# Experts' result rows in two halves by turns, stored from ScalarE's queue instead of SyncE's

## The reference, cut to what matters

```python
logits = x @ gate_w.T                      # 2048 tokens, 16 experts
vals, idx = jax.lax.top_k(softmax(logits), 2)
gate_out = (x @ g.T).reshape(bs, 16, 112)
up_out = (x @ u.T).reshape(bs, 16, 112)
h = jax.nn.silu(gate_out) * up_out
out = jnp.einsum('bei,hei,be->bh', h, d_r, w)
x = x + jnp.tanh(g_ffn[0]) * out
```

## Time and profile before

| what | value |
|---|---|
| median of three runs | 1417.61 us (1416.63 to 1420.79) |
| the profiled execution's own time | 1419.29 us |
| its span in the trace | 1417.6 us |
| busy PE, DVE, ACT, POOL | 89%, 55%, 39%, 41% |
| first down product of the experts to the last | 623.07 to 865.34 us, 39 tiles, 38 periods |

### The profile page before, as it was taken

How to read it: one execution, slowest core, us unless ns; L and a number is a source line. 1 busy time by engine, 2 the same in 40 slices (tenths; PEclk the granted TensorE clock), 3 DMA queues, 4 the chain that set the end, 5 groups by cost and what they waited for, 6 DMA issues and landing times. The chain is left out here.

```text
span 1417.6 us, 21035 instructions
## 1 busy us (share of the span) xinstructions
PE 1267.5 (89%) x6498; PEld 860.6 (61%) x6498; DVE 786.1 (55%) x2006; ACT 550.9 (39%) x913; POOL 579.5 (41%) x960
## 2 busy tenths in 40 slices
PE   3799999999976999999999994999999999658786
PEld 1354545445444854468777883888888889335443
DVE  2878888887863670023333333644554433449995
ACT  2544444444423400024343444232222232068884
POOL 4776868676732000012221222623222221157885
PEclk9999999999988999999999997999999999979999
DMA  5210212302003503038778865325323330121111
GB/s 192 78 71 30 89 59 94 128 30 104 0 1 139 221 1 125 21 95 260 253 224 260 270 211 192 119 91 133 106 90 120 120 90 31 59 68 45 59 59 74
DMA packets 52479, 156.36 MB, mean 110 GB/s; under 512 B 5952, under 2 KB 16192, under 8 KB 52288
## 3 DMA queue, kind: packets, MB, share of 16 engines
q1 hardware_dynamic: 39152, 113.60, 22.5%
q0 software_dynamic: 13264, 41.95, 10.7%
HBM read 113.06 MB, written 45.61 MB: 112 GB/s over the span
## 5 line engine op out<-in xcount | busy, mean ns | idle before, releaser
L1163 PEld LDWEIGHTS ex_bank<-ex_xT,ex_gu 128*112 128x112 f32 x1248 | 140.3, 177 | 25.2 <-issue 24.3
L1163 PE MATMUL ex_bank<-ex_xT,ex_gu 128*112 128x128 f32 x1248 | 144.0, 274 | 2.1 <-issue 1.0
L44 PE MATMUL xa_bank<-xa_fT_high,M_hi 128*128 128x256 f32 x512 | 145.6, 284 | 0.0
L45 PE MATMUL xa_bank<-xa_fT_low,M_hi 128*128 128x256 f32 x512 | 144.9, 283 | 0.0
L46 PE MATMUL xa_bank<-xa_fT_high,M_lo 128*128 128x256 f32 x512 | 144.9, 283 | 0.0
L52 PE MATMUL la_bank<-la_osum,la_tab 128*128 128x512 f32 x256 | 121.0, 618 | 15.8 <-POOL la_osum L297 14.6
L297 POOL TENSOR_TENSOR la_osum<-la_oprod 128x512 f32<-128x512 f32 x64 | 80.1, 1274 | 96.8 <-DVE la_oprod L476 96.8
L1051 POOL TENSOR_TENSOR ex_small<-listed,ex_small 128x1 int32<-128x1 int32 x42 | 8.0, 190 | 236.6 <-DVE Wk L1118 236.5
L1402 DVE SCALAR_TENSOR_TENSOR X<-ffn_row,weights,X 128x1024 f32<-128x1024 f32 x32 | 48.6, 1517 | 93.0 <-DMA ffn_row<-produced,xa_small_u 92.7
L44 PEld LDWEIGHTS xa_bank<-xa_fT_high,M_hi 128*128 128x128 f32 x512 | 98.4, 192 | 0.3
L45 PEld LDWEIGHTS xa_bank<-xa_fT_low,M_hi 128*128 128x128 f32 x512 | 98.4, 192 | 0.0
(11 more groups left out here) (278 smaller groups left out, 2907.5 us busy)
## 6 DMA issues: line engine op xcount, KB each, us to landing
produced<-Wk SPq DMA_DIRECT2D x39, 512.0 KB
ex_gu<-in_gate_up SPq DMA_DIRECT2D x16, 896.0 KB, 6.5
X<-in_x SPq DMA_DIRECT2D x8, 1024.0 KB, 7.6
la_v_raw<-in_ctx SPq DMA_DIRECT2D x16, 512.0 KB, 4.0
produced<-la_zeros SPq DMA_DIRECT2D x16, 512.0 KB, 4.7
normal<-rt_xn SPq DMA_DIRECT2D x16, 512.0 KB, 5.6
xa_fT<-in_ctx_T SPq DMA_DIRECT2D x8, 1024.0 KB, 5.5
xa_f<-in_ctx SPq DMA_DIRECT2D x8, 1024.0 KB, 4.9
```

The lines of the kernel that those rows point to most:

```text
L44: pe.matmul(out, a[0], b[0], start=first, stop=False)
L45: pe.matmul(out, a[0], b[1], start=False, stop=False)
L1163: m = pe.matmul(bank[half][0:INTER, 0:P], gu[:, slot, at:at + INTER], xT[:, k, :], start=(k == 0), stop=(k == KD - 1))
```

## The change

The result rows get two halves of a larger buffer, rows 2 and 3 of `W[1]`, chosen by g modulo 2. ScalarE issues the store of tile g itself, as the last thing in its turn, once store g-1 has landed and VectorE's copy of tile g is done. SyncE issues weights alone. The copy of tile g now waits for store g-2 instead of store g-1. A copy of one element, `taken`, carries this wait ahead of the real copy.

```diff
-        y, xs = W[1][:, 0, :], W[1][:, 1, :]
+        xs, results = W[1][:, 1, :], W[1][:, 2:4, :]
+        def half_of(eng, g):
+            return g % 2 * D if isinstance(g, int) else eng.snap(g % 2 * D)
+        def result(half, first=0, n=D):
+            return results.rearrange("p o d -> p (o d)")[:, bass.ds(half + first, n)]
...
-            sp.nop().then_inc(s["y_st"], 16)
...
-            for e in range(EXPERTS):
-                lo, hi = bounds(sp, e)
-                with sp.Fori(lo, hi) as g:
-                    row = sp.snap(g * P)
-                    sp.wait_ge(s["y_dve"], g + 2)
-                    sp.dma_start(produced[bass.ds(row, P), :], y[:]).then_inc(s["y_st"], 16)
-                if e + SLOTS < EXPERTS:
-
-                    load(e + SLOTS)
+            for e in range(SLOTS, EXPERTS):
+                done = bounds(sp, e - SLOTS)[1]
+                sp.wait_ge(s["y_dve"], done + 1)
+                load(e)
...
+            act.wait_ge(s["consts"], 1)
             act.nop().then_inc(s["y_act"], 1)
+            act.nop().then_inc(s["y_st"], 32)
...
+                row = g * P if isinstance(g, int) else act.snap(g * P)
+                half = half_of(act, g)
                 act.wait_ge(s["gate_done"], g + 1)
                 act.activation(sg[:], bank[0][0:INTER, 0:P], ACT.Silu).then_inc(s["silu_done"], 1)
                 rows_out(g + 1)
                 act.wait_ge(s["down_done"], g + 1)
                 act.wait_ge(s["y_st"], 16 * g + 16)
-                act.activation(y[:, 0:512], bank[4][:], ACT.Copy).then_inc(s["y_act"], 1)
-            act.wait_ge(s["y_st"], total * 16 + 16)
+                act.activation(taken[:], ident[0:1, 0:1], ACT.Copy)
+                act.activation(result(half, 0, 512), bank[4][:], ACT.Copy).then_inc(s["y_act"], 1)
+                act.wait_ge(s["y_st"], 16 * g + 32)
+                act.wait_ge(s["y_dve"], g + 2)
+                act.dma_start(produced[bass.ds(row, P), :], result(half)).then_inc(s["y_st"], 16)
+            act.wait_ge(s["y_st"], total * 16 + 32)
...
-                dve.tensor_copy(y[:, 512:1024], bank[5][:]).then_inc(s["y_dve"], 1)
+                dve.tensor_copy(result(half, 512, 512), bank[5][:]).then_inc(s["y_dve"], 1)
```

More of the change, by code:

```diff
@@ L1001, in experts @@
         hT = sb("hT", [INTER, P])
-        y, xs = W[1][:, 0, :], W[1][:, 1, :]
+        xs, results = W[1][:, 1, :], W[1][:, 2:4, :]
[3 more added lines that the diff above has]
+            return results.rearrange("p o d -> p (o d)")[:, bass.ds(half + first, n)]
         ident = sb("ident", [P, P])
+        taken = sb("taken", [1, 1])
         names = """one consts current rows_ready rows_held turned xT_act xT_dve gate_done up_half up_done silu_done hT_ready down_done
@@ L1125, in _ @@
             with dve.Fori(0, total) as g:
+                half = half_of(dve, g)
                 dve.wait_ge(s["silu_done"], g + 1)
```

## The result

| | kernel before | changed kernel |
|---|---|---|
| median of four runs | 1417.38 us | 1469.96 us |
| ratio, 95% interval | | 1.037 (1.033 to 1.041) |
| profiled execution, its span | 1419.29, 1417.6 us | 1467.23, 1465.4 us |
| first to last down product | 623.07 to 865.34, 242.3 us | 624.42 to 911.75, 287.3 us |

What follows compares the result with a forecast made beforehand. The prediction took the experts' stage as bound by TensorE's own work. Its terms, 3.7 + 2.6 - 0.2 = +6.1 us, against the median of 1417.6 gave 1424 us, with a range from 1413 to 1436 us.

Steps and rivals of the forecast that it cites:

- The ring: Chain through ScalarE and VectorE from one down product to the next: 6.44 us in every tile, stage +3.7 us.
- the loop's end to the table load: ScalarE's gap between issuing the store and its next table load, taken as 0.31 us.
- the starts of the two register-addressed copies: Gaps ahead of the result copies: 0.11 us from `taken` to ScalarE's copy, 0.15 us to VectorE's.
- Contention of the issue: At 13 tiles SyncE issues loads as ScalarE issues its store: 0.2 us each, +2.6 us in all.
- The wait for store g-1 ahead of the issue: ScalarE's wait for the previous store's landing before its DMA: free within 6.25 us, taken as 0, at most 7 us.
- The reasoning about queues: Store on its own queue beside loads: keeps 6.7 us, 5 us more at most, or passes waiting loads, nothing added.
- The table load: ScalarE's activation-table load ahead of Silu in each turn: 1.29 us with its gap, from the trace, not the skill's 2.66.
- (a): Rival, faster: chain between down products of 6.18 us, shorter than TensorE's 6.09 to 6.34 us tiles need; about 1412 us, chance 0.12.
- (b): Rival, a draw: chain between down products of 6.30 us, up to 3 us contention at switches; 1417 to 1420 us, chance 0.25.
- (c): Rival, slower by more: ScalarE's issue is dearer or meets the loads' issue; 1431 to 1434 us, chance 0.15.
- (d): Rival: stores still queue behind loads, 0.65 us in up to 11 tiles; 1424 to 1431 us, within the forecast's 0.48.
- the gain of the two halves: Copy g waits for store g-2 instead of g-1, so the stage loses 7.1 us of store waits if nothing else changed.

Runs made afterwards that it cites:

- run 8: Changed kernel without the 13 pairs of weight loads inside the stage and without the one-element copy `taken`: 1429.5 us, against 1431.8 us with that copy.
- run 2: Changed kernel with both halves kept, but SyncE issues the stores again, ahead of the loads in one queue: 1412.5 us, ratio 0.995.
- run 9: Changed kernel, but SyncE issues the loads only after ScalarE has issued the store, released by a counter behind the DMA: 1451.4 us, ratio 1.023.
- run 10: Changed kernel with all stores and loads on SyncE's queue, the loads issued ahead of each expert's last store: 1410.4 us, ratio 0.993.
- run 12: Changed kernel, but ScalarE issues the store of tile g-1 in turn g, behind its copy to xT, with the loop left whole: 1410.4 us, ratio 0.994.
- run 11: Changed kernel with only ScalarE's first turn taken out of its loop, so the table load leaves the loop: 1438.2 us, ratio 1.013.
- run 4: Changed kernel, but ScalarE issues store g-1 in turn g, behind its copy to xT, with the first turn out of the loop: 1410.95 us, ratio 0.994.
- run 13: Kernel before the change (one buffer, stores from SyncE) with ScalarE's first turn taken out of its loop: 1413.6 us, ratio 0.997.

## Why the prediction was wrong, point by point

- **The ring**: right as a mechanism, and near in size. Forecast 6.44 us, measured 6.66. The issue by ScalarE takes 0.35 us as on SyncE's queue, starts 0.18 us behind VectorE's copy (0.19 forecast), and the loop's end to the table load is 0.34 (0.31). The terms that were too small are the starts of the two register-addressed copies: 0.17 from `taken` to the copy instead of 0.11, and 0.28 instead of 0.15 to VectorE's. The 0.17 is hardly the price of `taken`, which run 8 puts at 0.03. The longer ring is +10.8 us over the stage instead of +3.7.
- **Contention of the issue**, +2.6 us: did not exist. The loads' issues take 0.33 and 0.43 us in the median beside ScalarE's, and ScalarE's own 0.40 at most.
- **The wait for store g-1 ahead of the issue**: this is the step that failed. The prediction set it at 0 with a bound of 7 us, from stores between 3.1 and 6.9 us. It cost 23.4 us, and another 11.0 through the clock. The bound was read from the wrong kind of row. The 3.1 us is a store ahead of the loads, and the 6.7 us one issued 4.1 us behind them, when they were well on their way. The changed kernel makes a third case that the trace before did not contain, store and loads starting at the same moment on two queues, and the prediction let the average DMA share of 0.74 stand for it. Counted from the loads' issue at 647.96, the late store of the earlier trace rows lands after 10.8 us; as a bound for a store that starts with them it would have held (9.4 measured).
- **The reasoning about queues** was upside down. On one queue the store issued ahead of the loads was sheltered from them (3.0 to 4.4 us in run 2); its own queue exposed it (7.4 to 8.5 us in 11 of 13 cases even when it is issued first, run 9). The changed kernel's DMA packets in the 2 us from 712.5 on, by queue (q1 SyncE, q10 ScalarE, q0 GpSimd):

```profile
q1 hardware_dynamic: 51, 0.37, 67.9%
q0 software_dynamic: 79, 0.26, 31.8%
q10 hardware_dynamic: 3, 0.01, 1.5%
```

  Between 1 and 3 us after its issue the store moves 3 packets of its 128, the loads move 51 and GpSimd's gather 79. In the 3.5 us from 714 on it is otherwise:

```profile
q1 hardware_dynamic: 146, 0.82, 63.6%
q10 hardware_dynamic: 106, 0.43, 29.8%
```

  The Trainium skill (DMA: Bandwidth & Descriptors, Queues, rings and completion order) has the engines take turns between the queues. The first stretch does not show even turns, the second comes near them. So this store is late in three parts: its first packet starts 2.5 us after the issue, it then shares with the loads, and its last few packets trail behind, the very last 0.3 us after the last one of gu, 8.4 us after the store's issue. In 9 of the 13 late stores the last packet follows gu's last one by 0.3 to 0.4 us. What holds the first and the last packets is open. The rule that more issuing engines bring no bandwidth (Rules for kernel authors) is not tested here: TensorE limits the best kernels, and run 10 with all on one queue and run 12 with two take the same 1410.4 us.
- **The clock** was not in the sum at all. In the changed kernel the seven stalls of 2.2 us and more are paid again in the following tile, and the six of 2.0 us and less are not. The length alone does not decide it. In run 9 the granted clock is 0.79 in the period behind a stall of 1.87 us; in run 11 it is 1.00 behind this one, and the down product takes 1.98 us:

```profile
768.47 1.98 PE L1189 MATMUL ex_bank<-ex_dn,ex_hT 112*128 112x512 f32 x4 [2.94 <-DVE ex_hT L1144]
```

- **The table load**: forecast 1.29 us with its gap, measured 712.19 to 713.48, 1.29. It was right to take the row. The 2.66 us of the Trainium skill (ScalarE: Activation LUTs, What ACT_TABLE_LOAD costs) are 1.28 for the load and 1.38 for a drain at a switch to another set of functions. The trace agrees with the first to the digit and shows no drain; whether these loads switch sets at all, no run shows.
- **Rivals**: (a) and (b) needed a ring of at most 6.30 us, which was 6.66. (c) named a slower ending, but by a dear issue or contention of issues, which both were not there; (d), stores that still land late, was the right rival with a fifth of its real price, and I had put it inside the forecast. Its sentence that it "cannot take back the gain of the two halves" was wrong: the wait had moved from the copy to the issue, where the halves cover nothing.

## What to carry to other kernels

Keep an engine that computes off any wait for a landing: a second buffer helps only if the wait for the transfer before is not put in front of the same engine's next work. If a compute engine must issue a store, put the issue where that engine is idle anyway (run 12). For a DMA that will start together with others on another queue, take as bound the landing of the whole group from its first issue (10.8 us here, for 9.4 measured). And give a stall of TensorE a second price, for the clock that can fall behind it: 11.0 us behind seven stalls here.

## What the runs showed of the hardware that I had not expected

- A store of 512 KB issued 0.15 us behind an 896 KB load on another queue landed up to 9.4 us after its issue, against at most 5.1 us without loads; with 448 KB beside it, at most 6.7. Issued 0.43 us ahead of the load, it still landed up to 8.5 us after its issue. Why the first load weighs so much more than the bytes behind it is open.
- A copy whose address comes from a register started 0.18 us later behind its releaser on VectorE (0.28 against 0.10), and on ScalarE 0.15 us later behind the down product (2.25 us in run 8, where no `taken` stands ahead of it, against 2.10).
- ScalarE's loop has no activation-table load in its turns, 1.28 us each, once its first turn is written out ahead of it (runs 4, 11 and 13); its busy time fell from 107.8 to 62.2 us over the stage in run 4.
- After idling 3.1 us TensorE ran at a mean granted clock of 0.61 over 8.5 us, and its down product took 3.78 us instead of 1.98; after idling 2.9 us in run 11 its clock stayed at 1.00.
